# The sixth product of a seven-product matrix multiply accumulates on a ScalarE copy of the first

## The reference, cut to what matters

```python
q = x @ Wq; k = x @ Wk; v = x @ Wv
attn = softmax(einsum('btd,bTd->btT', q, k) * V ** -0.5)
attn_out = einsum('btT,bTd->btd', attn, v) @ Wp + bp
cms_out = gelu(attn_out @ cW1 + cb1) @ cW2 + cb2 + target_embed      # 512 -> 2048 -> 512
modifier = gelu(concat([attn_out, cms_out], -1) @ mW1 + mb1) @ mW2 + mb2   # 1024 -> 2048 -> 512
out = clip(x + cms_out + modifier, 0.0, 1.0)
```

## Time and profile before

| | us |
|---|---|
| median of 3 runs | 2171.19 (2169.8 to 2171.62) |
| the profiled execution's own time | 2169.23 |
| its span in the trace | 2167.4 |
| TensorE busy | 2130.0 (98% of the span) |
| VectorE busy | 1421.1 (66%) |
| ScalarE busy | 864.5 (40%) |
| mean granted TensorE clock | 0.996 of full speed |

### The profile page before, as it was taken

One profiled execution on the slowest core, in us unless ns is written; L12 is line 12 of the kernel. 1 busy time (PEld: TensorE's weight loads), 2 busy tenths in 40 slices (PEclk: granted clock), 3 DMA queues, 4 the chain that ended last, 5 costly groups with the idle time before them and its releaser, 6 DMA issues.

```text
span 2167.4 us, 28421 instructions
## 1 busy us (share of the span) xinstructions
PE 2130.0 (98%) x10112; PEld 1785.5 (82%) x10112; DVE 1421.1 (66%) x2249; ACT 864.5 (40%) x1484; POOL 363.4 (17%) x356
## 2 busy tenths in 40 slices
PE   9999999999999999999999999999999999999996
PEld 7888888888888888888878888888888888888885
DVE  6587775566567777655667778555655777756564
ACT  5454443333354444333345445333334544433331
POOL 0011021210401111221231111211031111121204
PEclk9999999999999999999999999999999999999998
DMA  8111212114421122112730111122262011121135
GB/s 318 72 30 59 78 40 68 68 64 149 109 78 49 49 74 69 44 58 68 241 110 30 59 49 64 59 68 68 93 180 93 30 51 57 68 68 64 49 104 135
DMA packets 46281, 178.05 MB, mean 82 GB/s; under 512 B 5954, under 2 KB 10050, under 8 KB 39234
## 3 DMA queue, kind: packets, MB, share of 16 engines
q1 hardware_dynamic: 46146, 176.25, 25.1%
HBM read 159.45 MB, written 16.78 MB: 81 GB/s over the span
## 4 chain that ended last, share of the span: by engine, by line
PE 63%; DVE 3%; DMA 2%; issue 1%; POOL 1%; SPq 1%; ACT 1%; DVEq 0%; POOLq 0%; ACTq 0%
PE psum L482 59%; DMA rolep<-roles_in 1%; DMA raw_u<-up_in 1%; PE psum L764 1%; PE psum L730 1%; PE psum L556 1%; PE psum L578 1%; DVE wup L1061 0%; SPq L322 0%; SPq L321 0%; POOL yt L465 0%; POOL yt L467 0%; DVE xs L1061 0%; DVE stats L1366 0%; DVE yt L1364 0%
## 5 line engine op out<-in xcount | busy, mean ns | idle before, releaser
L482 PE MATMUL psum<-hs,wd 128*128 128x512 f32 x3072 | 716.8, 389 | 0.0
L482 PEld LDWEIGHTS psum<-hs,wd 128*128 128x128 f32 x3072 | 576.3, 188 | 120.9 <-issue 1.4
L1225 DVE TENSOR_TENSOR acc<-psum,acc 128x512 f32<-128x512 f32 x480 | 311.9, 683 | 111.5 <-PE psum L482 111.3
L482 PE MATMUL psum<-cop,wsm 128*128 128x512 f32 x1416 | 354.7, 389 | 0.0
L482 PE MATMUL psum<-aop,wsm 128*128 128x512 f32 x1320 | 332.9, 389 | 0.0
L482 PEld LDWEIGHTS psum<-cop,wsm 128*128 128x128 f32 x1416 | 265.8, 188 | 55.2
L482 PE MATMUL psum<-aop,wsc 128*128 128x512 f32 x1320 | 310.7, 389 | 0.0
L482 PEld LDWEIGHTS psum<-aop,wsm 128*128 128x128 f32 x1320 | 247.8, 188 | 51.4
L482 PEld LDWEIGHTS psum<-aop,wsc 128*128 128x128 f32 x1320 | 247.5, 188 | 51.4
L941 ACT ACTIVATE hs<-psum,bias 128x512 fp32r<-128x512 f32 x88 | 60.8, 691 | 445.6 <-PE psum L482 445.6
L1061 DVE TENSOR_TENSOR hs<-zt,hs 128x512 fp32r<-128x512 f32 x256 | 180.2, 704 | 85.6 <-ACT zt L942 85.6
(11 more groups left out here) (119 smaller groups left out, 2357.1 us busy)
## 6 DMA issues: line engine op xcount, KB each, us to landing
w1m<-m_in SPq DMA_DIRECT2D x32, 1024.0 KB, 4.9
rolep<-roles_in SPq DMA_DIRECT2D x64, 384.0 KB, 4.7
w1c<-c_in SPq DMA_DIRECT2D x32, 512.0 KB, 3.6
w<-c_in SPq DMA_DIRECT2D x32, 512.0 KB, 3.7
w<-m_in SPq DMA_DIRECT2D x32, 512.0 KB, 3.6
fw<-fused SPq DMA_DIRECT2D x6, 2048.0 KB, 11.1
fused<-fw SPq DMA_DIRECT2D x4, 2048.0 KB, 7.5
raw_u<-up_in SPq DMA_DIRECT2D x4, 1536.0 KB, 8.9
```

What stands on the lines that cost most here:

```text
L482: mm = nc.tensor.matmul(out, lhs(a), rhs(b), start=(start and n == 0), stop=(stop and n == total - 1), skip_group_check=reopened)
L1225: nc.vector.tensor_tensor(dst, d_out[o][:, :], dst, ALU.add).then_inc(acc_done, 1)
```

## The change

In the 7-product units ScalarE copies P1 from bank A into bank B (not to `zt`), and P6 accumulates on that copy. Everything later in bank B then holds P1 already. So `make_u2` becomes a ScalarE copy of bank B to `zt` (`copy_u2`), `make_z21` goes and ScalarE's Gelu reads H10 straight from bank B, and of the two sums of `make_z22` one is left, with P5 first copied to `zt` by ScalarE (`copy_p5`). VectorE keeps `make_z22` (one sum) and `make_z12`. P6 now waits for the copy of P1. In the lists of ScalarE the copy of P1 of unit u + 1 moves to the end of unit u, ahead of H01, where u is a 7-product unit; for units 1 and 9 it stays at the start of the unit. H01 of the plain unit 0 moves from bank 4 to bank 1.

```diff
 # TensorE, term
-                first = i in (P1, P5, P6) and which == 0
+                first = i in (P1, P5) and which == 0
...
-                    if i == P6:
-                        if u == NG + 1:
-                            pe.wait_ge(h_hi[H01], n)
-                        elif u % NG > 1:
-                            pe.wait_ge(z21_done, e)
                 if not first:
-                    if i == P2:
+                    if i in (P6, P2):
                         pe.wait_ge(p1_copied, e + 1)
                     if i == P7:
-                        pe.wait_ge(u2_done, e + 1)
+                        pe.wait_ge(u2_copied, e + 1)
                     if i == P4:
-                        pe.wait_ge(u3_done, e + 1)
+                        pe.wait_ge(z22_done, e + 1)
                     if i == P3:
-                        pe.wait_ge(z22_done, e + 1)
+                        pe.wait_ge(p5_copied, e + 1)
 # ScalarE
             def copy_p1(p, u):
                 act.wait_ge(prod[P1], strassen(p, u) + 1)
-                act.wait_ge(h_lo[H10], UNITS * p + u)
-                nc.scalar.activation(zt[:, 0, :], bank_a()[:, :], ACT.Copy).then_inc(p1_copied, 1)
+                act.wait_ge(h_hi[H01 if plain(u - 1) else H10], UNITS * p + u)
+                nc.scalar.activation(bank_b()[:, :], bank_a()[:, :], ACT.Copy).then_inc(p1_copied, 1)
+            def copy_p5(p, u):
+                act.wait_ge(prod[P5], strassen(p, u) + 1)
+                act.wait_ge(h_lo[H11], UNITS * p + u)
+                nc.scalar.activation(zt[:, 2, :], bank_c(u)[:, :], ACT.Copy).then_inc(p5_copied, 1)
+            def copy_u2(p, u):
+                act.wait_ge(prod[P6], strassen(p, u) + 1)
+                act.wait_ge(h_lo[H01], UNITS * p + u)
+                nc.scalar.activation(zt[:, 1, :], bank_b()[:, :], ACT.Copy).then_inc(u2_copied, 1)
...
+                elif h == H10:
+                    act.wait_ge(prod[P4], strassen(p, u) + 1)
+                    act.wait_ge(h_lo[H10], n)
                 else:
-                    act.wait_ge({H11: z22_done, H10: z21_done, H01: z12_done}[h], strassen(p, u) + 1)
+                    act.wait_ge({H11: z22_done, H01: z12_done}[h], strassen(p, u) + 1)
...
-                    copy_p1(p, u)
+                    if plain(u - 1):
+                        copy_p1(p, u)
+                    copy_p5(p, u)
                     for i in (P4, P3):
                         weight_part(p, u, i)
+                    copy_u2(p, u)
                     hidden(p, layer, u, H00)
...
+                    if nxt and not plain(u + 1):
+                        copy_p1(p, u + 1)
                     hidden(p, layer, u, H01)
 # VectorE
-            def make_u2(p, u): ...
             def make_z22(p, u):
                 dve.wait_ge(prod[P7], e + 1)
-                dve.wait_ge(h_lo[H11], UNITS * p + u)
-                nc.vector.tensor_tensor(zt[:, 2, :], bank_b()[:, :], zt[:, 0, :], ALU.add).then_inc(u3_done, 1)
-                dve.wait_ge(prod[P5], e + 1)
-                dve.wait_ge(u3_done, e + 1)
-                nc.vector.tensor_tensor(zt[:, 2, :], bank_c(u)[:, :], zt[:, 2, :], ALU.add).then_inc(z22_done, 1)
-            def make_z21(p, u): ...
+                dve.wait_ge(p5_copied, e + 1)
+                nc.vector.tensor_tensor(zt[:, 2, :], bank_b()[:, :], zt[:, 2, :], ALU.add).then_inc(z22_done, 1)
```

More of the change, by code:

```diff
@@ L207, in cond_seq_kernel @@
         prod = [sem(f"prod{i}") for i in range(7)]
-        p1_copied, u2_done, u3_done = sem("p1_copied"), sem("u2_done"), sem("u3_done")
-        z22_done, z21_done, z12_done = sem("z22_done"), sem("z21_done"), sem("z12_done")
+        p1_copied, p5_copied, u2_copied = sem("p1_copied"), sem("p5_copied"), sem("u2_copied")
+        z22_done, z12_done = sem("z22_done"), sem("z12_done")
         h_hi = [sem(f"h_hi{i}") for i in range(4)]
@@ L279, in plain_bank @@
         def plain_bank(kind):
-            return {H00: ps[0], H10: ps[6], H01: ps[1], H11: ps[7]} if kind else {H00: ps[2], H10: ps[3], H01: ps[4], H11: ps[5]}
+            return {H00: ps[0], H10: ps[6], H01: ps[1], H11: ps[7]} if kind else {H00: ps[2], H10: ps[3], H01: ps[1], H11: ps[5]}
         def h_place(h):
@@ L287, in h_source @@
                 return plain_bank(kind_of(u))[h]
-            return {H00: bank_a(), H11: zt[:, 2, :], H10: zt[:, 0, :], H01: zt[:, 1, :]}[h]
+            return {H00: bank_a(), H11: zt[:, 2, :], H10: bank_b(), H01: zt[:, 1, :]}[h]
         def h_raw(h):
@@ L594, in block_products @@
                     elif h == H01:
-                        pe.wait_ge(z21_done, strassen(p, u))
+                        pe.wait_ge(h_hi[H10], n)
                     else:
@@ L655, in term @@
                     (lambda a, k=k: slot(u, i)[:, a, (2 * which + k) * P:(2 * which + k + 1) * P], lambda c, k=k: src[:, i, c, k, :], None)
-                    for k in range(2)], first, last, i in (P2, P7, P4, P3))
+                    for k in range(2)], first, last, i in (P6, P2, P7, P4, P3))
                 if last:
@@ L1190, in hidden @@
                 minus(hs[:, b, LO, m, :], h_raw(h), hs[:, b, HI, m, :]).then_inc(h_lo[h], 1)
[L1192 to L1197, removed]
             def make_z22(p, u):
@@ L1201, in make_z22 @@
                 dve.wait_ge(prod[P7], e + 1)
-                dve.wait_ge(h_lo[H11], UNITS * p + u)
-                nc.vector.tensor_tensor(zt[:, 2, :], bank_b()[:, :], zt[:, 0, :], ALU.add).then_inc(u3_done, 1)
-                dve.wait_ge(prod[P5], e + 1)
-                dve.wait_ge(u3_done, e + 1)
-                nc.vector.tensor_tensor(zt[:, 2, :], bank_c(u)[:, :], zt[:, 2, :], ALU.add).then_inc(z22_done, 1)
-            def make_z21(p, u):
-                dve.wait_ge(prod[P4], strassen(p, u) + 1)
-                nc.vector.tensor_tensor(zt[:, 0, :], bank_b()[:, :], zt[:, 0, :], ALU.add).then_inc(z21_done, 1)
+                dve.wait_ge(p5_copied, e + 1)
+                nc.vector.tensor_tensor(zt[:, 2, :], bank_b()[:, :], zt[:, 2, :], ALU.add).then_inc(z22_done, 1)
             def make_z12(p, u):
                 dve.wait_ge(prod[P3], strassen(p, u) + 1)
-                dve.wait_ge(u2_done, strassen(p, u) + 1)
+                dve.wait_ge(u2_copied, strassen(p, u) + 1)
                 nc.vector.tensor_tensor(zt[:, 1, :], bank_c(u)[:, :], zt[:, 1, :], ALU.add).then_inc(z12_done, 1)
@@ L1287, in mlps @@
                         weight_part(p, u, i)
-                    make_u2(p, u)
                     add(p, layer, u - 1, 0, *every)
@@ L1298, in mlps @@
                         weight_part(p, u + 1, P4 if u + 1 == NG else P7)
-                        make_z21(p, u)
                         make_z12(p, u)
```

## The result

| | before | after |
|---|---|---|
| median, us | 2170.9 (2169.8 to 2171.62) | 2193.07 (2192.0 to 2194.39) |
| profiled execution, us (span) | 2169.23 (2167.4) | 2192.87 (2191.1) |
| ratio of the runs | | 1.0103, 95% interval 1.0085 to 1.0120 |

A forecast was written before the change was run, and what follows sets the result against it. TensorE's unbroken matmul stream was taken to bound the kernel. Stops 17.1 + clock 5.2 - pass ends 0.6 = 21.7 us on the median of 2171.19 gave 2192.9 us, 1.0% slower; 8-in-10 range 2186.5 to 2199.

The forecast's parts named there:

- What bounds it: In 7-product units TensorE never stops, so work taken off VectorE buys nothing by itself; only a new wait matters.
- Off the path: 7-product units: VectorE loses 116 us of busy time, ScalarE gains 65 us, both beside TensorE's stream; cost 0.
- P7, P4, P3 and SP's loads: 7-product units: these products' waits have room, and SP's load, about 1.2 us later in kind 1, stays covered; cost 0.
- Units 2 to 7 and 10 to 15: P6 waits for the copy of P1 with 0.40 us spare in kind 0, 1.76 us in kind 1; cost 0.
- the open price: Length of ScalarE's copy of P1 into PSUM, shown by no row: taken as 0.58 us, bounds 0.40 and 0.69.
- The stop in unit 1: Once per pass P6 waits for a copy late in ScalarE's list: 3 x 4.18 + 4.53 = 17.1 us.
- The clock: After each of the four unit 1 stops the granted clock falls, costing 1.3 us each, 5.2 us in all.
- The end of each pass: Last unit: VectorE's low part of the down weights starts 0.15 to 0.2 us sooner per pass; -0.6 us.
- The clock that stays up: Rival: the unit 1 stops come but the clock doesn't fall after them; 2187.7 us, chance 13%.
- A late copy in units 2 to 7: Rival: the copy is late in kind 0 too, 24 units paying 0.1 to 0.3 us each; about 2198 us, chance 18%.
- Not slower: Rival: unit 1's copy of P1 ends 4.2 us sooner, so no stop; 2162.8 to 2170.6 us, chance 4%.

The follow-up runs named there:

- P6 later: Changed kernel, but in unit 1 TensorE does P6 after the down-projection of unit 0's first token block instead of before: 2170.04 us, ratio 1.0000.
- the last experiment: P6 later kernel with two of VectorE's three removed sums put back as sums of no use, Gelu H10 waiting for them: 2168.97 us, ratio 0.9997.
- the filled kernel: Changed kernel with 18 matmuls of no use ahead of P6 in unit 1: 2185.54 us, ratio 1.0071.
- the kernel with the wait alone: Kernel before the change with one wait added: P6 in unit 1 waits for the copy of P1, which it doesn't read: 2194.86 us, ratio 1.0111.
- 9 matmuls in the stop: Changed kernel with 9 matmuls of no use ahead of P6 in unit 1: 2188.38 us, ratio 1.0086.
- the two repairs: Changed kernel with unit 1's P1 copied right after Gelu H01 in unit 0 (2170.62 us), or with P6 after the first down-projection (2170.04 us).

## Why the prediction was right

**What bounds it.** That TensorE's stream is the path held: where no new wait stopped it (P6 later, and the same with the sums back), units 0 to 7 came out equal to 0.01 us, whatever ScalarE and VectorE did beside them.

**Off the path: 0.** The time is right; the busy times were a little off. VectorE lost 100 us where 116 were forecast and ScalarE gained 59 where 65 were. A row's length holds some overlap with its neighbour: the 112 sums of the last experiment add up to 83.1 us by their rows and added 74 us of busy time.

**P7, P4, P3 and SP's loads: 0.** The chain after has no break at them, and the kind 1 stage isn't longer in any pass. In unit 10 SP's load starts at 873.91 us, 70.67 us after the first matmul of unit 8; before it was 861.95 less 792.50, 69.45. So it moved back by the 1.2 us that were forecast. GpSimd's first combination ends at 880.44 and ScalarE takes it at 884.00, 3.6 us to spare where it was 5.0. The cover held, with less room.

**Units 2 to 7 and 10 to 15: 0.** Right, and the steps of the working can be read in the changed kernel's second pass:

```profile
678.12 6.96 PE L482 MATMUL psum<-aop,wsc 128*128 128x512 f32 x30
...
680.57 0.40 ACT L906 ACTIVATE wsc<-w1c 128x256 fp32r<-128x256 f32 x1
...
680.88 0.67 ACT L950 ACTIVATE hs<-psum,bias 128x512 fp32r<-128x512 f32 x1
681.45 0.67 ACT L951 ACTIVATE zt<-psum,bias 128x512 f32<-128x512 f32 x1
...
682.40 0.58 ACT L919 ACTIVATE psum<-psum 128x512 f32<-128x512 f32 x1 [0.28 <-PE psum L482]
...
684.92 5.60 PE L482 MATMUL psum<-hs,wd 128*128 128x512 f32 x24
```

ScalarE's weight at 680.57, H10 from 680.88 on, straight from the bank, and the copy at 682.40, where P1 had ended at 678.12 + 18 x 0.2267 = 682.20: the 0.20 us of latency. ScalarE was ready 0.28 us earlier. The copy into PSUM was the open price. The groups by line, mean ns in the column after the busy time, in the changed kernel:

```profile
L924 ACT ACTIVATE zt<-psum 128x512 f32<-128x512 f32 x56 | 32.9, 588 | 27.1 <-PE psum L482 27.1
L919 ACT ACTIVATE psum<-psum 128x512 f32<-128x512 f32 x56 | 32.6, 582 | 106.2 <-PE psum L482 106.2
```

and the copy of P1 in the kernel before, into SBUF:

```profile
L923 ACT ACTIVATE zt<-psum 128x512 f32<-128x512 f32 x56 | 32.2, 575 | 0.0
```

It is 0.582 us into PSUM (L919), as good as the 0.58 taken. Into SBUF the same copy took 0.575, and that of P5 (L924) 0.588. The Trainium skill ("ScalarE: Activation LUTs", section "Step-by-step: what each stage is for") says that writing to PSUM is the faster; these rows don't show it, since the differences are 0.007 us one way and 0.006 us the other.

**The stop in unit 1: 16.7 us against 17.1.** The first, second and fourth pass were right at 4.18 us, which the filled kernel shows as the 4.18 us that its stage is longer. The third was given 4.53 because the copy stood 0.35 us later there in the trace of before; in the changed kernel its break is 3.93 us like the others. The step that failed here is that the change leaves VectorE's and ScalarE's chain up to this copy as it was. The late start belongs to the third pass of the old lists: the kernel with the wait alone, another execution, has it too (4.28 us and not 3.93), and the changed kernel and those made from it don't. Why the change took the 0.35 us away is open. In the other passes P6's row starts 4.09 us later than before and the stage is another 0.09 us longer; the 0.18 us of the prediction hold both, since they were taken from the end of a row.

**The clock: 9.1 us against 5.2.** The mechanism was right, at each of the four stops. The size of this term wasn't: it was given as 2 to 6.4 us, and 9.1 lies outside. I had taken 3.4 us of slow clock for each fall, from the one fall before with work behind it, and at most 1.6 us of loss. In three of the four passes it stayed down for 6.8 us, of which about 5 us had work in them: (160.64 + 160.42 + 160.32) - 3 x (153.80 + 4.18) = 7.4 us for three, and 1.6 for the second pass, which had 3.4. The kernel with the wait alone has four more such stops, two of each kind. By windows and by the lengths of units 0 to 7:

| stop of 4.2 us (4.5 in the one marked *) | clock fell | clock down, us | lost by it, us |
|---|---|---|---|
| changed kernel, first pass | 1.2 us before TensorE resumed | 6.8 | 2.7 |
| second | 0.9 us after | 3.4 | 1.6 |
| third | 1.6 us before | 6.8 | 2.4 |
| fourth | 1.9 us before | 6.8 | 2.3 |
| wait alone, first pass | 0.1 us after | 3.4 | 1.6 |
| second | 0.2 us before | 3.4 | 1.6 |
| third * | 1.2 us before | 6.8 | 2.6 |
| fourth | 1.2 us before | 6.8 | 2.7 |

The window of the third pass of the wait alone shows what a long one costs, 13 matmuls of 0.427 us and not 0.227, 0.2 us more each:

```profile
1192.10:1197.60 5.50, 5.48 (x13) 4.34 (x14) 2.56 (x5) 0.53 (x2) 0.25 (x1) 0.50 0.31 98
```

All eight sort the same way: where TensorE stood still for 1.2 us or more after the fall, the clock was down for 6.8 us, and where it was back within 0.2 us or had already resumed, for 3.4. The fall with 9 matmuls in the stop (0.6 us after TensorE resumed) and the one of before (0.3 us before) were of the short kind too. No run varied this by itself, so that it is the cause isn't shown. The Trainium skill ("TensorE: Matmul & The Clock Gate", section "Part 1: The HAM clock gate") says that idling halves the array's rate and activity restores it; the eight stops agree, and the filled kernel, in which TensorE never idles there, has no fall there.

**The end of each pass: -0.6 us.** Measured -0.63 by the stage of units 8 to 15. It stayed with two of the sums put back, so it isn't theirs; that it is H10's, as forecast, wasn't tested. The last unit after:

```profile
1042.86 1.06 ACT L913 ACTIVATE wd<-w 128x1024 fp32r<-128x1024 f32 x1 [1.51 <-PE psum L482]
...
1043.95 1.23 DVE L1075 TENSOR_TENSOR wd<-w,wd 128x1024 fp32r<-128x1024 f32 x1 [0.46 <-ACT wd L913]
```

As forecast, VectorE's low part now waits for ScalarE's, 0.46 us, and starts 0.03 us after it ends; in the earlier trace rows it started 0.21 us after, on VectorE's own account.

**Sum.** 16.7 + 9.1 - 0.6 - 1.5 = 23.7 us by the traces, where 21.7 was forecast. So on the profiled execution the forecast was 2.0 us too low: the clock term was 3.9 us too small, and 0.4 of stops and 1.5 of untouched stages went the other way. Between the medians the difference was 22.2 us, 0.5 above the forecast, and the median of before moved by 0.3 us as a run was added. That the forecast median was met within 0.2 us is luck in the terms; what was right is the place, the length of the stops and that the clock falls after them. By the runs the clock's part is some 7 us, give or take 5, so they alone couldn't tell 9.1 from 5.2.

**Rivals.** The clock that stays up fell with the eight stops. A late copy in units 2 to 7 fell with the stages of the two kernels in which P6 of unit 1 comes later, equal to the hundredth. "Not slower" needed a copy 4.2 us sooner, and that is just what the two repairs give: with it, or with P6 behind the down-projection, the ratios are 1.0006 and 1.0000, each with 0.0009 either way: no gain and no loss is shown. No kernel here beats the one before.

## What to carry to other kernels

When a consumer's wait moves ahead of the work that used to hide the producer, look for the one place where the producer's list is different (here the first unit after another kind of unit) and work out the time there by itself; in the steady units it fitted with 0.3 us to spare. Relief of an engine that isn't late anywhere buys nothing: 74 us of VectorE's work put back left the units' lengths as they were. And a stop of TensorE of some 4 us was paid one and a half times here ((16.7 + 9.1) / 16.7), since the clock is down when it resumes or soon after; the cheap repair is to move one entry in either list.

## What the runs showed of the hardware

The fall of the clock after a stop had no fixed price: 1.6 us with the clock down for 3.4 us, and 2.3 to 2.7 us where it was down for 6.8. The long kind came in five of eight stops of some 4.2 us, those in which TensorE stood still for another 1.2 us or more after the fall. Stops of 0.5 and 1.8 us brought no fall in four places each, stops of 2.1 us one in four, stops of 4.2 us eight in eight. A matmul accumulating on what ScalarE wrote in the bank takes no longer than any other (units 0 to 7 at 153.79 us with and without), and ScalarE's copy of 128x512 from PSUM took 0.582 us into PSUM and 0.575 or 0.588 us into SBUF.
